# W1 loaded by column blocks, ids spread by a K=1 matmul, the setup of G01 reordered, and a different warm-up of TensorE

## The reference

```python
x = x + x @ W_base.T + scaling[i0] * ((((x @ Wt.T) @ A[i0].T) @ B_w[i0].T) @ Wp.T)   # 4 adapters, rank 16
x = x + x @ W.T + scalings[i1] * ((x @ A1[i1].T) @ Bm[i1].T)                          # 8 adapters, rank 16
x = x + einsum('bct,bcd->bdt', x, weights2[i2])      # mixes the 64 tokens of a sequence, 8 matrices
x = x + einsum('bct,bcd->bdt', x, weights3[i3])      # the same, 200 matrices
```

## Time and profile before

| | |
|---|---|
| median of 3 runs | 172.35 us (172.17 to 172.74) |
| the profiled execution | 172.37 us |
| its span, first to last instruction | 170.2 us |
| TensorE (PE) busy, of the span | 163.6 us, 96% |
| DVE, ACT, POOL busy | 54%, 28%, 51% |
| DMA | 28.75 MB, mean 169 GB/s |

### The profile page before, as it was taken

One profiled execution on the slowest core, in us unless ns is written; L12 is line 12 of the kernel. 1 busy time (PEld: TensorE's weight loads), 2 busy tenths in 40 slices (PEclk: granted clock), 3 DMA queues, 4 the chain that ended last, 5 costly groups with the idle time before them and its releaser, 6 DMA issues.

```text
span 170.2 us, 6468 instructions
## 1 busy us (share of the span) xinstructions
PE 163.6 (96%) x2348; PEld 125.0 (73%) x2348; DVE 91.1 (54%) x212; ACT 48.5 (28%) x96; POOL 86.7 (51%) x194
## 2 busy tenths in 40 slices
PE   5889999999999999999999999999999999999992
PEld 5669467678786878687868886877778687868761
DVE  4195975899770846263636645563666180617010
ACT  3142426244230602240223024220503060214021
POOL 4410477764675648475737674756454053608200
PEclk9999999999999999999999999999999999999998
DMA  4799942119550594077309531953394059006406
GB/s 141 252 329 321 282 177 85 33 60 331 190 192 27 168 322 145 23 208 293 131 15 294 209 137 70 285 178 116 123 311 161 31 155 337 2 0 250 123 9 242
DMA packets 16614, 28.75 MB, mean 169 GB/s; under 512 B 3862, under 2 KB 3990, under 8 KB 16598
## 3 DMA queue, kind: packets, MB, share of 16 engines
q1 hardware_dynamic: 14294, 23.31, 41.8%
q0 software_dynamic: 2304, 5.25, 9.1%
HBM read 18.85 MB, written 9.70 MB: 168 GB/s over the span
## 4 chain that ended last, share of the span: by engine, by line
PE 91%; DMA 3%; DVE 1%; SPq 1%; issue 1%; ACT 1%; POOL 0%; DVEq 0%
PE o_ps L751 65%; PE y_ps L751 12%; PE z_ps L751 8%; DMA wb_sb<-in_L_cond_W_base_dram 3%; PE p_ps L751 3%; PE y_ps L764 1%; SPq L231 1%; PE y_ps L811 1%; DVE g L552 0%; PE p_ps L853 0%; DVE b_by L546 0%; ACT o_sb L486 0%; PE p_ps L824 0%; PE z_ps L811 0%; PE p_ps L811 0%
## 5 line engine op out<-in xcount | busy, mean ns | idle before, releaser
L751 PE MATMUL o_ps<-g,yy 128*128 128x512 f32 x384 | 92.1, 395 | 0.0
L751 PEld LDWEIGHTS o_ps<-g,yy 128*128 128x128 f32 x384 | 70.8, 188 | 16.1 <-issue 0.8
L339 POOL COPY u_sel<-u_tab 128x64 f32 x128 | 32.3, 258 | 41.3 <-PE z_ps L751 31.5
L318 POOL DMA_INDIRECT w_all<-in_L_cond_weights_dram,w_rows x32 | 31.8, 994 | 9.6 <-issue 9.6
L631 DVE COPY y_all<-y_ps 128x512 f32<-128x512 f32 x32 | 20.6, 686 | 15.0 <-PE y_ps L751 14.9
L673 DVE COPY o_sb<-o_ps 128x512 f32<-128x512 f32 x15 | 9.7, 687 | 34.5 <-PE o_ps L751 34.5
L426 ACT ACTIVATE yy<-y_all 128x512 fp32r<-128x512 f32 x32 | 19.7, 632 | 16.5 <-DVE y_all L631 16.1
L638 DVE TENSOR_TENSOR yy<-y_all,yy 128x512 fp32r<-128x512 f32 x32 | 21.2, 701 | 3.0 <-ACT yy L426 2.7
L327 POOL DMA_INDIRECT v_sel<-v_table,v_rows x16 | 17.5, 1094 | 6.2 <-issue 6.2
L445 ACT ACTIVATE o_sb<-o_ps 128x512 f32<-128x512 f32 x16 | 8.7, 595 | 37.9 <-PE o_ps L751 37.9
L751 PE MATMUL y_ps<-p_now,x_raw 64*64 64x64 f32 x1024 | 18.6, 221 | 0.0
(11 more groups left out here) (115 smaller groups left out, 104.5 us busy)
## 6 DMA issues: line engine op xcount, KB each, us to landing
x_raw<-in_x_dram SPq DMA_DIRECT2D x16, 512.0 KB, 4.7
out_dram<-o_sb SPq DMA_DIRECT2D x14, 512.0 KB, 5.4
w_sb<-in_L_cond_W_dram SPq DMA_DIRECT2D x4, 256.0 KB, 3.6
wb_sb<-in_L_cond_W_base_dram SPq DMA_DIRECT2D x4, 256.0 KB, 7.1
wp_sb<-in_L_cond_Wp_dram SPq DMA_DIRECT2D x2, 512.0 KB, 6.3
wt_sb<-in_L_cond_Wt_dram SPq DMA_DIRECT2D x1, 1024.0 KB, 8.9
v_table<-v_tab SPq DMA_DIRECT2D x1, 1024.0 KB, 5.7
out_dram<-o_sb SPq DMA_DIRECT2D x4, 256.0 KB, 2.3
```

What stands on the lines that cost most here:

```text
L318: pool.indirect_dma_start(out=w3_all[:, j, :], out_offset=None, in_=w3_flat, in_offset=bass.IndirectOffsetOnAxis(ap=w3_rows[:, j:j + 1], a ...
L339: nc.gpsimd.tensor_copy(u_sel[u][:, :, b, RANK * part:RANK * part + RANK], u_tab[:, :, bass.ds(e, 1), :].rearrange("p k a r -> p k (a r)") ...
L751: return nc.tensor.matmul(dst, lhsT, rhs, start=start, stop=stop)
```

## The change

It touches the setup only; the loop of turns is as before.

- **W1** is loaded as four column blocks of 128 rows by 128 columns by four row groups (`w1_sb[:, k, :, :]`), pieces of 512 bytes. One block completes one bank, so `flip_w1(k)` gives g1_k. SP's order becomes W1 block 0, W_base 0, W1 1, W_base 1, W1 2, W1 3, Wp, W_base 2, A1, A0, W2, s0, B0, Wt, W_base 3, s1, B1.
- **Ids** come by four 256-byte DMAs on ACT's queue onto one partition. DVE casts them to float32r, a matmul with a row of ones (K=1, N=256) spreads them over 128 partitions into `z_ps`, and DVE copies them to `ids`. The five other id loads, with their spreads, leave SP's queue.
- **Warm-up**: DVE sets a tile `blank` to zero at its start, and TensorE runs 18 float32 matmuls of `blank` (128x128) by 64 of its columns, then, after `flip_w1(0)`, six more.
- **Order on TensorE**: 18 warm-up matmuls, `flip_w1(0)`, six warm-up matmuls, the four high matmuls of G01, `flip_w1(1)`, the rest of step 0, the ids matmul, `flip_w1(2)`, step 1, `flip_w1(3)`, the transposes of Wp, A1, A0, W2, then `g01_step(2)`, and `vu` as before. After `v0g1` come `mix(0)`, half of `g01_step(3)`, a wait for both `copy_y` of DVE, the four V products, the rest of step 3, turn 0.
- **Order on DVE, ACT and POOL**: `low_wb(2)` ahead of the copy of wpT_3; `place_w2(1)` directly behind `place_w2(0)`; `add_w3(1)`, `find_v_rows`, `v0g1`, both `copy_y` and `low_y(0, 0)` ahead of the V sums, which go 3, 2, 1, 0; `high_y(0, 0)` ahead of `read_g01(0)`. POOL issues the first gather ahead of `plus_wb(2)` and four more ahead of `plus_wb(3)`.

```diff
-            for c in range(KC):
-                sp.dma_start(w1_sb[:, c, :], w1_rows[:, c, :]).then_inc(w1_in[c], 16)
-            for k in range(2):
-                load_wb(k)
-            sp.dma_start(ids[:, 2, :], e3_ids.partition_broadcast(PART)).then_inc(e3_in, 16)
-            for n, t in enumerate((e0_ids, e1_ids, e2_ids)):
-                sp.dma_start(code_ids[:, n, :], t.partition_broadcast(1)).then_inc(code_in, 16)
+            for k in range(KC):
+                sp.dma_start(w1_sb[:, k, :, :], w1_rows[:, k, :, :]).then_inc(w1_in[k], 16)
+                if k < 2:
+                    load_wb(k)
...
+            for n, t in enumerate((e0_ids, e1_ids, e2_ids, e3_ids)):
+                act.dma_start(ids_row[:, n, :], t.partition_broadcast(1)).then_inc(ids_in, 16)
...
+            low_g1(0)
+            dve.wait_ge(ids_in, 64)
+            nc.vector.tensor_copy(ids_f[:, :, :], ids_row[:, :, :]).then_inc(ids_f_set, 1)
+            low_g1(1)
             low_wb(1)
+            dve.wait_ge(ids_spread, 1)
+            nc.vector.tensor_copy(ids[:, :, :].rearrange("p n b -> p (n b)"), z_ps[:, 0:4 * BATCH]).then_inc(ids_set, 1)
...
             place_w2(0)
+            place_w2(1, w2_next)
...
-            place_w2(1, w2_next)
+            add_w3(1, w3_next)
+            find_v_rows()
             dve.wait_ge(setup_act, ACT_DONE["v0g1"])
             read("v0g1", v0g1[0:R0, :], bank_of("v0g1")[0:R0, :], v0g1_low[:, :], ALU.add)
+            for u in range(2):
+                copy_y(0, u)
+            low_y(0, 0)
...
-                    nc.tensor.transpose(o_ps[3][:, 0:PART], ident[:, :], ident[:, :])
+                    mm(o_ps[3][:, 0:SEQ], blank[:, :], blank[:, 0:SEQ], True, True)
+            pe.wait_ge(blank_set, 1)
+            keep_warm(18)
...
+            flip_w1(0)
+            keep_warm(6)
+            g01_high()
+            flip_w1(1)
             g01_step(0)
+            pe.wait_ge(ids_f_set, 2)
+            mm(z_ps[:, 0:4 * BATCH], ones_row[:, :], ids_f[:, :, :].rearrange("p n b -> p (n b)"),
+               True, True).then_inc(ids_spread, 1)
+            flip_w1(2)
             g01_step(1)
+            pe.wait_ge(ids_set, 1)
+            flip_w1(3)
...
+            g01_step(2)
             free_bank("vu")
...
-            g01_step(2)
-            pe.wait_ge(p_set, 1)
+            pe.wait_ge(setup_act, ACT_DONE["gu1"])
+            mix_ready(0, 0)
+            mix(0)
+            g01_step(3, range(0, 2))
+            pe.wait_ge(yf_set, 2)
             pe.wait_ge(setup_dve, DVE_DONE["cross_odd"])
```

More of the change, by code:

```diff
@@ L63, in build @@
         ident2 = sb("ident2", [PART, SEQ])
+        blank = sb("blank", [PART, PART])
         owner = sb("owner", [PART, E1])
-        ids = sb("ids", [PART, 3, BATCH], I32)
-        code_ids = sb("code_ids", [1, 3, BATCH], I32)
+        ids = sb("ids", [PART, 4, BATCH], I32)
+        ids_row = sb("ids_row", [1, 4, BATCH], I32)
+        ids_f = sb("ids_f", [1, 4, BATCH], F32R)
+        ones_row = sb("ones_row", [1, PART], F32R)
+        one = sb("one", [1, PART])
         code_part = sb("code_part", [1, 3, BATCH], I32)
@@ L190, in build @@
                  "a1T": 0, "a0T": 2, "w2T": 1, "vu": 6, "vuT": 0, "gu1T": 2, "v1": 1, "cross": 6,
[2 rows of a table removed]
-        ACT_STEPS = ["g1_0", "g1_1", "wb_high_1", "g1_2", "g1_3", "wpT_0", "wpT_2", "a1T", "wb_high_2", "wb_high_3",
+                 "gu1": 2, "v0g1": 6,
+                 "g01_0": 4, "g01_1": 5, "v_0": 1, "v_1": 2, "v_2": 0, "v_3": 6, "g01_2": 3, "g01_3": 7}
+        ACT_STEPS = ["g1_0", "g1_1", "wb_high_1", "g1_2", "g1_3", "wpT_0", "wb_high_2", "wpT_2", "a1T", "wb_high_3",
                      "vu", "v0T", "gu1T", "v1", "vuT", "gu1", "v0g1", "v0g1_both",
@@ L405, in _ @@
                 read_g1(k)
-            for s in range(0, KC, 2):
-                read(f"wpT_{s}", wpT[:, s, :], bank_of(f"wpT_{s}"))
+            read("wpT_0", wpT[:, 0, :], bank_of("wpT_0"))
+            high_wb(2)
+            read("wpT_2", wpT[:, 2, :], bank_of("wpT_2"))
             read("a1T", a1T[:, 0, :, :].rearrange("p k r -> p (k r)"), bank_of("a1T"))
-            for k in range(2, KC):
-                high_wb(k)
+            high_wb(3)
             read("vu", vu[:, :], bank_of("vu"))
@@ L572, in low_g1 @@
                 read_low(f"g1_{k}", g1[:, 1, k, :], bank_of(f"g1_{k}"), g1[:, 0, k, :])
+            nc.vector.memset(blank[:, :], 0.0).then_inc(blank_set, 1)
+            link(nc.vector.memset(one[:, :], 1.0))
+            nc.vector.tensor_copy(ones_row[:, :], one[:, :]).then_inc(ids_f_set, 1)
             dve.wait_ge(ident_set, 2)
@@ L607, in _ @@
             last.then_inc(code_set, 1)
+            low_g1(3)
             def copy(name, dst, src):
@@ L611, in copy @@
                 nc.vector.tensor_copy(dst, src).then_inc(setup_dve, 1)
-            for s in range(1, KC, 2):
-                copy(f"wpT_{s}", wpT[:, s, :], bank_of(f"wpT_{s}"))
+            copy("wpT_1", wpT[:, 1, :], bank_of("wpT_1"))
+            low_wb(2)
+            copy("wpT_3", wpT[:, 3, :], bank_of("wpT_3"))
+            scale(E0, b0_in, b0_sb, b0_now, s0_sb)
             copy("a0T", a0T[:, :, :].rearrange("p k r -> p (k r)"), bank_of("a0T")[:, 0:KC * R0])
@@ L622, in _ @@
                 read("w2T", w2T[SEQ * b:SEQ * b + SEQ, :, :].rearrange("p g (a j) -> p g a j", j=W2J), w2_bank, eye, ALU.add)
-            for k in range(2, KC):
-                low_wb(k)
+            low_wb(3)
             def copy_y(i, u):
@@ L773, in g01_part, with g01_high @@
                 return last
-            def g01_step(k, blocks=range(KC)):
[L777 to L781, removed]
+            def g01_high():
+                pe.wait_ge(setup_act, ACT_DONE["g1_0"])
+                pe.wait_ge(setup_dve, DVE_DONE["wb_high_0"])
+                for t in range(KC):
+                    g01_part(0, t, ((0, 0),))
+            def g01_step(k, blocks=range(KC)):
                 pe.wait_ge(setup_dve, max(DVE_DONE[f"g1_{k}"], DVE_DONE[f"wb_low_{k}"]))
@@ L1002, in _ @@
                    True, True).then_inc(setup_ps, 1)
-            g01_step(3, range(0, 2))
-            pe.wait_ge(setup_dve, DVE_DONE["v_1"])
-            mix_ready(0, 0)
-            mix(0)
             g01_step(3, range(2, KC))
```

88 lines of the change are left out of this document (42 added, 46 removed), and 2 rows, old and new, of the table ORDER.

## The result

The changed kernel takes 179.95 us (median of 6 runs, 179.71 to 180.3) where the kernel before takes 172.73 (median of 6, 172.17 to 173.04): a ratio of 1.0425, 95% interval 1.0402 to 1.0448. It is 7.2 us slower, far outside the range of 171.2 to 174.2. Some executions of a kernel fall into a slower state; ratios compare the runs outside it, while medians are of all runs. The profiled execution took 179.93 us, its span is 177.9, 7.7 more than before.

What follows compares the result with a forecast made beforehand. TensorE, busy for 96% of the span, bounds the kernel, so the start of turn 0's `reduce(0)` decides. G01 starting 1.8 us earlier, +1.9 behind it, gives +0.1 on 172.37: 172.5 us, range 171.2 to 174.2.

Steps and rivals of the forecast that it cites:

- Part 1: TensorE's start: 36 warm-up pieces at 0.11 us end at 5.03, so G01's first matmul starts 1.8 us earlier.
- rival 3: TensorE's warm-up: weight loads stretch with the clock, pieces cost 0.22 us until it rises; 174.2 us, chance 0.19.
- G: First matmul of G01 on TensorE, counted at its weight load: forecast at 7.0 us, before at 8.81.
- late clock: TensorE's start: the clock rises late behind zeros; chance 0.04.
- Part 2: Stretch from G01's first matmul to turn 0's `reduce(0)`: terms added or taken sum to +1.9 us.
- The low part's wait: TensorE's wait for the low part of g1_0 early in G01, covered by `flip_w1(1)`: -0.55 us.
- `g01_step(2)` hides the wait for A0: Moved ahead of `vu` on TensorE, its 12 matmuls hide the wait for the copy of A0: -0.28 us.
- place_w2(1): Directly behind `place_w2(0)`, it makes DVE late to v0T's low part, so B1's transposes wait: +0.8 us (0 to 1.3).
- SP's queue: SP's loads, gathers and x: Wt and the last W_base block land before they are needed; hidden, no cost.
- Rival 1: TensorE's warm-up: loads hidden beneath other pieces, matmuls cost 0.213 then 0.107 us; 0.8 less, 171.7 us, chance 0.12.
- Rival 2: Ahead of B1's transposes: DVE isn't late, so the +0.8 is gone; 171.7 us, chance 0.17.
- Rival 4: W1's 512-byte pieces load slowly, the last W_base block holds DVE's row by 0.5 to 1.0 us; 173.3, chance 0.10.

Runs made afterwards that it cites:

- e5: Changed kernel with 16 and 6 transposes of the identity as warm-up, on a chip without stalls: 173.03 us, ratio 1.0041 to the kernel before.
- e6: Changed kernel with 9 and 3 float32 warm-up matmuls of zeros moving 128 columns: 172.73 us, ratio 1.0024 to the kernel before.
- e2: Changed kernel with the blank tile set to 1.2345678 in place of 0: 187.34 us, ratio 1.0412 to the kernel before.
- e3: Changed kernel with transposes of the tile of zeros as warm-up: 179.52 us, ratio 1.0005 to the kernel before, on a stalling chip.
- e7: Changed kernel with identity transposes as warm-up and `place_w2(1)` back behind the `cross` steps: 174.58 us, ratio 1.0149 to the kernel before.
- e8: Changed kernel with identity transposes as warm-up and turn 1's x load ahead of the V table's store: 172.42 us, ratio 0.9997 to the kernel before.
- e1: Changed kernel with 16 and 6 transposes of the identity as warm-up, on a stalling chip: 180.28 us, ratio 1.0021 to the kernel before.
- e9: Changed kernel with warm-up weight tiles of 64 columns, 64 moving, counts unchanged: 181.17 us beside 180.09 of the kernel before, stalling chip, no interval.
- e13: Changed kernel with half the warm-up matmuls (9 and 3), form unchanged, on another stalling chip than e10: 182.69 us, ratio 1.0104 to the kernel before.
- e4: Kernel before with its 16 warm-up transposes replaced by 18 float32 matmuls of `blank`: 184.5 us, ratio 1.0287 to the kernel before.
- e10: Changed kernel with half the warm-up matmuls (9 and 3), form unchanged, on a stalling chip: 181.55 us, ratio 1.0073 to the kernel before.
- e14: Same kernel as e12, run again on a stalling chip: 180.95 us, ratio 1.0022 to the kernel before.
- e15: Changed kernel with identity-transpose warm-up, turn 1's x ahead of the V table's store, W_base block 3 ahead of Wt: 179.66 us, ratio 0.9972 to the kernel before.
- e12: Changed kernel with e6's warm-up, turn 1's x ahead of the V table's store, W_base block 3 ahead of Wt: 179.81 us, ratio 1.0006 to the kernel before.

## Why the prediction was wrong

**Part 1 failed**, at the sentence "I take it that the load doesn't stretch with the clock, and each piece costs 0.11 us at either level". It came from two loads started 0.063 apart. Only the first step of that row is so short, and the 15 behind it are 0.213 each; a first pair says nothing of the rate of 36, as the changed kernel shows again, with 0.166 for its first step and 0.213 for all others. The pieces took 0.213. That was the upper bound that I had named for the case "if they stretch" and put into rival 3.

**The forecast and rival 3 shared a second assumption**, and it made even rival 3 too small: that the clock would rise at 4.7 to 5.4, TensorE being at work without a gap. It rose in step 0 of G01, between 15.7 and 15.9 us. TensorE was busy from 1.14 on, with what turned out to be pieces whose pace is set by the load. Forty-eight pieces at 0.213 are 10.2 us for the 5.3 reckoned, so G came at 12.08 for 7.0, far outside the 6.5 to 7.4 that I had set as the sign of a wrong forecast. Then G01's start ran at the lower level: 1.6 of the 2.2 us that the stretch from G to `vu` took beyond the forecast. That stretch also runs 0.4 over in e5 and e6 (13.82 for 13.4). In e5, 0.2 of it lies at step 2, which takes 2.95 from the last transpose of W2 to `vu`, where the old 0.39 and the sum's 2.67 - 0.28 make 2.78; the rest lies between G and there, in the flips and the ids matmul, and I have not parted it further. The 0.04 given to a late clock named the wrong cause: e2 and e3 show that zeros have no part in it.

The Trainium skill (TensorE: Matmul & The Clock Gate, Part 4: PE-mode transpose) says that transposes don't count as busy for the clock, by which the old warm-up would have been the useless one. In the trace of e3, and of the kernel before, the clock rose behind 16 transposes. By the formula of the Trainium skill (TensorE: Matmul & The Clock Gate, LDWEIGHTS) a load of 128 columns is 107 ns; the runs agree at 2.4 GHz with 0.109 us for float32 and show 0.213 at 1.2 GHz.

**Part 2, term by term.** The low part's wait is gone, as reckoned. `g01_step(2)` hides the wait for A0: its place now shows an "issue" gap only, but this gap is as long (0.35 at the loads), so the 0.28 came in part at most. **place_w2(1)** was sized at 0.8 and costs 0.1 in the changed kernel: there DVE's low part of v0T starts 6.29 behind `vu` (33.93), before it was 6.17 (24.63). The mechanism was right, B1's transposes do wait for DVE, and the size was wrong at both ends. In e5 the two placings take 5.5 us (21.31 to 26.81) where I had put 5.9, and `vu` starts 6.4 behind the last flip where I had put 6.2, so DVE is only some 0.2 late. (The terms of the sum give F + 12.31 for TensorE, not 12.35, which changes nothing.) In e6 the stretch is 1.1 over, but there the reason is another: DVE waits 1.07 for W_base block 3. The landing itself came when I had reckoned it (POOL's sum starts at 19.20); DVE now asks for the block at 19.29, since G is 1.0 earlier than forecast. e7 shows the other half, which I hadn't priced: left where it was, the placing would have cost 1.9 from `vu` to `reduce(0)`, 2.0 at the V products less 0.2 at B1. The wait of 0.4 for `copy_y` is there (0.36), and the last stretch took 9.89 for 10.05.

**SP's queue was called hidden, and isn't.** x of turn 1 stands behind the store of the V table. SP's issues in the changed kernel, and before:

```profile
46.18 0.36 SPq L278 DMA_DIRECT2D v_table<-v_tab  x1
46.58 2.83 SPq L255 DMA_DIRECT2D x_raw<-in_x_dram  x2
```
```profile
36.88 0.36 SPq L278 DMA_DIRECT2D v_table<-v_tab  x1
37.29 3.33 SPq L255 DMA_DIRECT2D x_raw<-in_x_dram  x2
```

The store was issued 1.56 us ahead of `reduce(0)` before, and is now issued 1.22 us behind it, since the V sums come after both `copy_y`. x lands that much later, 6.85 us after its issue, and the second reduce waits 0.74 for it. I had moved the V sums in my sum without moving the queue that hangs on them. This step of the instruction list I had put at nothing; it costs 0.75 us by e8.

**Rival 1** (loads hidden) is refuted, by 0.213 for 64 moving columns. **Rival 2** (DVE isn't late) came near: of the 0.8 only 0.12 came in the changed kernel and 0.15 in e5. **Rival 4** (512-byte pieces) isn't what happened: POOL's sum on W1's second block started at 6.54 us, in time even for the forecast, and from 6 to 9 us the DMA engines moved 359 GB/s:

```profile
6.54 0.45 POOL L353 TENSOR_TENSOR w_sb<-w_sb,ident 128x128 f32<-128x128 f32 x1 [1.60 <-DMA w_sb<-in_L_cond_W_dram]
...
8.16 0.46 POOL L353 TENSOR_TENSOR w_sb<-w_sb,ident 128x128 f32<-128x128 f32 x1 [0.42 <-DMA w_sb<-in_L_cond_W_dram]
9.03 0.46 POOL L353 TENSOR_TENSOR w_sb<-w_sb,ident 128x128 f32<-128x128 f32 x1 [0.41 <-DMA w_sb<-in_L_cond_W_dram]
```
```profile
6.00:9.00 3.00, 3.00 (x16) 3.00 (x16) 0.21 (x1) 0.00 (x0) 1.37 (x3) 1.00 1.11 359
```

Blocks follow each other by 0.87 us, between the 0.70 and 1.19 of the bounds.

In sum: the warm-up's length and its clock are shown by the timelines of e1 to e6, e9 and e13, and by e5 they make up all but 0.4% of the loss. With a warm-up that works, the reordering brings `reduce(0)` 0.35 to 0.6 us forward and gives it back at x of turn 1 (e8). That e6 and e5, at 172.73 and 173.03, end near the forecast of 172.5 is luck: in e6 G came 1.0 earlier than forecast, the two stretches up to B1 took 0.7 more, and the wait for x had no term. What raises the clock, beyond the forms tried here, stays open.

## What to carry to other kernels

Take for a warm-up a form that a trace has shown to raise the clock. Here float32 matmuls with 128 moving columns for 128 loaded, or 64 for 64, and transposes did; with 64 moving for 128 loaded the pieces ran at the load's pace and the clock stayed at 1.2 GHz. Price a stream of pieces by the larger of load and move at the level of the clock at which it runs, and take the rate from a long stream, never from its first pair. When a result moves on an engine, follow the DMA that waits for it and everything queued behind that DMA.

## What the runs showed of the hardware

- A float32 load of 128 columns takes 0.213 us at 1.2 GHz (after) and 0.109 at 2.4; one of 64 columns 0.107 at 1.2 GHz (e9). It isn't hidden by 64 moving columns, and 128 moving columns add nothing to it (e6).
- In the changed kernel TensorE was busy without a gap from 1.14 on and stayed at 1.2 GHz up to 15.7 us. In all five profiles with this form of warm-up (after, e2, e4, e10, e13) the clock rose inside G01: at about 10.5 (e13), 11.2 (e10), 13.4 (e4), 15.3 (e2) and 15.8 us (after). In e4 it rose only 0.8 us behind G, but there 16 transposes of W1 stand between the warm-up and G. In the twelve others it rose between 4.2 (e6, e14) and 7.5 us (e15), and there the moment differs from run to run of one kernel: e14 had it ahead of W1's transposes (0.60 for the four), e12, which is the same kernel, behind them (1.06), and G moved from 6.29 to 6.97. Such a spread makes one profile of a start a weak witness for differences under 1 us.
- The granted clock in the windows read 1.00 all through the slow stretch, as in the row from 6.00 to 9.00 above. Only the lengths of pieces showed it.
